# The first chunk of the attention stage: its stream rows in a buffer of their own, its result rows with one load per tile, its statistics tile by tile

## What is computed

```
x = x + 0.5 * ffn(layernorm(x))      # first expert stage
x = x + attn(layernorm(x))           # attention stage
x = x + 0.5 * ffn(layernorm(x))      # second expert stage

def ffn(x):                          # 8 experts, the 2 best of each row
    scores = x @ gate_w.T + gate_b + bias
    top, idx = top_k(scores, 2); gates = softmax(top)
    y_e = silu(x @ w1[e].T + b1[e]) @ w2[e].T + b2[e]
    return sum of gates * y_idx over the two
def attn(x):                         # 6 heads of 128, rows in order of time
    q, k, v = conv4(x @ Wq), conv4(x @ Wk), conv4(x @ Wv)
    alpha, beta = sigmoid(x @ Wa), sigmoid(x @ Wb)
    state = alpha * rotate(state, dq) + beta * rotate(v, k)     # a scan over the rows
    out = rotate(state, -q)
    return (out * rsqrt(mean(out**2)) * rms_w * silu(x @ Wg)) @ Wo
```

## Time and profile before

| | |
|---|---|
| median of 3 runs | 895.51 us (894.84 to 895.96) |
| the profiled execution | 895.87 us |
| its span in the trace | 894.1 us |
| TensorE's mean granted clock | 0.922 of full |
| PE, DVE, ACT, POOL busy | 83%, 70%, 39%, 26% |
| first expert stage ends (last matmul) | 267.5 us from the span's start |
| first matmul of the attention stage | 290.8 us |

### The profile page before, as it was taken

One profiled execution on the slowest core, in us unless ns is written; L12 is line 12 of the kernel. 1 busy time (PEld: TensorE's weight loads), 2 busy tenths in 40 slices (PEclk: granted clock), 3 DMA queues, 4 the chain that ended last, 5 costly groups with the idle time before them and its releaser, 6 DMA issues.

```text
span 894.1 us, 13749 instructions
## 1 busy us (share of the span) xinstructions
PE 737.8 (83%) x4128; PEld 406.8 (45%) x4129; DVE 622.1 (70%) x1009; ACT 348.1 (39%) x600; POOL 236.3 (26%) x222
## 2 busy tenths in 40 slices
PE   8527699999990898997999999999529999999910
PEld 5215455555550444443444444444316565656600
DVE  6886755566654269999989998995775555555545
ACT  5714333434320546445644654532703323333300
POOL 3115644444520101101211011021113434444300
PEclk9859999999995899899999999999859999999965
DMA  9936568865425430610441201363836733333269
GB/s 321 385 111 207 186 223 317 322 243 176 143 83 199 99 89 21 121 49 0 88 78 24 60 12 25 120 166 128 311 112 223 255 107 117 117 106 117 84 223 374
DMA packets 45305, 137.25 MB, mean 153 GB/s; under 512 B 5840, under 2 KB 5840, under 8 KB 41936
## 3 DMA queue, kind: packets, MB, share of 16 engines
q1 hardware_dynamic: 27888, 86.38, 26.8%
q0 software_dynamic: 17376, 50.34, 20.5%
HBM read 85.32 MB, written 51.38 MB: 153 GB/s over the span
## 4 chain that ended last, share of the span: by engine, by line
PE 70%; DVE 15%; DMA 5%; issue 4%; ACT 3%; SPq 1%; POOL 0%; DVEq 0%; POOLq 0%; ACTq 0%
PE bank L615 59%; PE bank L609 4%; PE bank L687 3%; DMA space<-y_rows 2%; PE bank L804 2%; DVE space L1469 1%; DVE space L1466 1%; DVE space L1259 1%; DVE bst L1250 1%; SPq L477 1%; DMA y_rows<-space,slot_dst 1%; DVE space L1316 1%; DMA space<-x_in 1%; DMA space<-xn_rows,slot_src 1%; PE bank L738 1%
## 5 line engine op out<-in xcount | busy, mean ns | idle before, releaser
L615 PE MATMUL bank<-space 128*128 (+3 forms) x2958 | 581.0, 349 | 44.5 <-DVE space L1320 25.6
L615 PEld LDWEIGHTS bank<-space 128*128 128x128 f16 (+1 forms) x2958 | 274.3, 99 | 296.2 <-issue 37.7
L541 POOL DMA_INDIRECT y_rows<-space,slot_dst x78 | 99.7, 1278 | 158.2 <-DVE space L1380 158.2
L1361 DVE TENSOR_TENSOR space<-bank,space 128x512 f16<-128x512 f32 x78 | 54.0, 692 | 84.8 <-issue 43.2
L537 POOL DMA_INDIRECT space<-xn_rows,slot_src x78 | 76.3, 978 | 130.4 <-PE bank L609 70.0
L977 ACT ACTIVATE space<-space 128x352 f32<-128x352 f32 x78 | 38.7, 496 | 177.3 <-DVE space L1367 174.8
L1367 DVE SCALAR_TENSOR_TENSOR space<-bank,space 128x352 f32<-128x352 f32 x78 | 40.9, 524 | 64.0 <-PE bank L615 49.1
L609 PE MATMUL bank<-ident,space 128*128 128x128 f32 x440 | 67.6, 284 | 12.4 <-DMA space<-xn_rows,slot_src 10.5
L982 ACT ACTIVATE space<-bank 128x384 f16<-128x384 f32 x78 | 38.3, 491 | 77.9 <-PE bank L687 76.7
L1380 DVE TENSOR_SCALAR space<-bank,slot_gate 128x512 f32<-128x512 f32 x78 | 58.5, 750 | 12.9 <-PE bank L615 10.3
L1466 DVE SCALAR_TENSOR_TENSOR space<-space,cang 128x512 f32<-128x512 f32 x84 | 63.0, 750 | 5.5 <-ACT space L1051 3.3
(11 more groups left out here) (172 smaller groups left out, 697.4 us busy)
## 6 DMA issues: line engine op xcount, KB each, us to landing
space<-ffn_w SPq DMA_DIRECT2D x8, 1472.0 KB, 10.0
w_saved<-space SPq DMA_DIRECT2D x8, 1472.0 KB
space<-w_saved SPq DMA_DIRECT2D x8, 1472.0 KB, 9.5
space<-y_rows SPq DMA_DIRECT2D x40, 256.0 KB, 6.0
xn_rows<-space SPq DMA_DIRECT2D x8, 1024.0 KB, 6.1
space<-x_in SPq DMA_DIRECT2D x7, 1024.0 KB, 5.3
space<-att_w SPq DMA_DIRECT2D x12, 518.0 KB
space<-y_rows POOLq DMA_DIRECT2D x6, 1024.0 KB, 9.3
```

What stands on the lines that cost most here:

```text
L541: gp.indirect_dma_start(y_rows, bass.IndirectOffsetOnAxis(ap=slot_dst[:, t:t + 1], axis=0), yo[:, t % 2], None).then_inc(y_st[t % 2], 16)
L615: last = pe.matmul(dst, a, b, start=(n == 0), stop=(n == len(terms) - 1))
L1361: v.tensor_tensor(xl[:, par], bank[par][:, :], xh[:, par], ALU.subtract).then_inc(m_xl, 1)
```

## The change

1. Chunk 0's stream rows get a range of their own, `group_rows[0]`, which begins where the second `oh` buffer (odd chunks) begins. The other chunks keep `xgrp`. SP no longer waits for `m_yo` before `group_in(0)`.
2. `y_first` of a tile comes with one load of both result rows (128 x 2 x 512) and not with two.
3. SP issues chunk 1's `group_in` right behind these loads and ahead of `group_out(0)`, without a wait, since `xgrp` isn't used by chunk 0.
4. DVE takes each tile's statistics (`bn_stats`) right behind its two additions.
5. ACT waits for chunk 0's store (`x1_st`) before it first writes the second `oh` buffer, at u = 3.

```diff
+        first_at = lay.at
         oh.append(lay([2 * PAIRS, CH], F16))
         ol.append(lay([2 * PAIRS, CH], F16))
         ...
+        group_rows = [Layout(first_at)([TPC, D])] + [xgrp] * (NCH - 1)
...
             slot_weights()
-            sp.wait_ge(m_yo, SLOT_TILES + 2)
             def group_in(c):
-                sp.dma_start(xgrp, rows4(x_in, c)).then_inc(cg_in, 16)
+                sp.dma_start(group_rows[c], rows4(x_in, c)).then_inc(cg_in, 16)
...
             def next_group_in(c):
-                sp.wait_ge(x1_st, 16 * c)
-                sp.wait_ge(c_xn, TPC * c)
+                if c > 1:
+                    sp.wait_ge(x1_st, 16 * c)
+                    sp.wait_ge(c_xn, TPC * c)
                 group_in(c)
...
             for i in range(TPC):
-                for k in (0, 1):
-                    sp.dma_start(y_first[:, k, i], y_rows[bass.ds(k * T + i * P, P), :]).then_inc(yf_in[i], 16)
+                sp.dma_start(y_first[:, :, i], y_rows[0:2 * T, :].rearrange("(k n p) d -> n p k d", k=2, p=P)[i]).then_inc(yf_in[i], 16)
+            next_group_in(1)
             group_out(0)
-            next_group_in(1)
...
             def gate_high(u):
                 ...
+                if u == PAIRS:
+                    act.wait_ge(x1_st, 16)
...
             def first_rows():
                 v.wait_ge(cg_in, 16)
                 for i in range(TPC):
-                    v.wait_ge(yf_in[i], 32)
-                    seq(v.tensor_tensor(xgrp[:, i], xgrp[:, i], y_first[:, 0, i], ALU.add))
-                    v.tensor_tensor(xgrp[:, i], xgrp[:, i], y_first[:, 1, i], ALU.add).then_inc(c_sum, 1)
+                    v.wait_ge(yf_in[i], 16)
+                    seq(v.tensor_tensor(group_rows[0][:, i], group_rows[0][:, i], y_first[:, 0, i], ALU.add))
+                    v.tensor_tensor(group_rows[0][:, i], group_rows[0][:, i], y_first[:, 1, i], ALU.add).then_inc(c_sum, 1)
                     v.wait_ge(c_sum, i + 1)
+                    ch(v.bn_stats(bst[:, i], group_rows[0][:, i]))
+                ch.wait()
...
             def attention():
                 first_rows()
-                variance(xgrp)
+                moments()
```

More of the change, by code:

```diff
@@ L413, in group_out @@
                     sp.wait_ge(cy_in[1], 16 * c)
-                sp.dma_start(rows4(x_rows, c), xgrp).then_inc(x1_st, 16)
+                sp.dma_start(rows4(x_rows, c), group_rows[c]).then_inc(x1_st, 16)
             def next_group_in(c):
-                sp.wait_ge(x1_st, 16 * c)
-                sp.wait_ge(c_xn, TPC * c)
+                if c > 1:
+                    sp.wait_ge(x1_st, 16 * c)
+                    sp.wait_ge(c_xn, TPC * c)
                 group_in(c)
@@ L1019, in normalise @@
                     act.wait_ge(c_xt, TPC * c + i - 1)
-                act.activation(xnt[:, i % 2], xgrp[:, i], ACT.Identity, scale=rstd[:, 0, 0, i:i + 1],
+                act.activation(xnt[:, i % 2], group_rows[c][:, i], ACT.Identity, scale=rstd[:, 0, 0, i:i + 1],
                                bias=rstd[:, 0, 1, i:i + 1]).then_inc(c_xn, 1)
```

## The result

| | before | after |
|---|---|---|
| median | 895.65 us (894.84 to 896.36, 5 runs) | 891.86 us (891.17 to 892.38, 5 runs) |
| profiled execution | 895.87 us | 891.86 us |
| its span | 894.1 us | 890.1 us |
| TensorE's mean granted clock | 0.922 | 0.919 |

The ratio is 0.9959, with a 95% interval of 0.9947 to 0.9971: the change makes the kernel 3.8 us faster (2.6 to 4.7). I had forecast 891.3 us within 889.2 to 894.0.

A forecast was written before the change was run, and what follows sets the result against it. PE sets the pace, but idles from 267.5 to 290.8 us behind the last scatter and statistics. Gains of 3.54 + 0.7 = 4.24 us take 895.87 to 891.6, forecast as 891.3 against the median, range 889.2 to 894.0.

The forecast's parts named there:

- The last scatter, 3.54 us: First expert stage's end: without chunk 0's load ahead of it, the last `y_rows` scatter takes 3.54 us less, bounds 0 and 3.54.
- The twin: Same last scatter ending the second expert stage, with no load beside it: 2.73 us, used to price the first at 6.27.
- The load's new place, 0: Chunk 0's load behind the last attention weights, about 229.5: PE should not notice, cost 0, at most 1.2 us.
- One load per tile, 0 (0.46 either way): Result rows after the scatter: first tile's data arrives 0.46 us earlier to 0.46 later, taken as 0.
- Statistics tile by tile, 0.7: DVE, first addition to fourth statistics: 8.6 us instead of 9.33, including 0.2 wait; gain 0.7, bounds 0.3 and 1.1.
- The sum: From the experts to the attention: 3.54 + 0.7 = 4.24 us off the path, so the attention starts that much sooner.
- PE, ACT and POOL work behind it only follows: Work after the shortened link: no gain or loss of its own, the attention just starts 4.24 us sooner.
- 2.05 us either way: Rival, PE's clock at the restart after idling: granted earlier (889.3, chance 0.08) or later (893.3, chance 0.09).
- a half-clock stretch more than before: Sign in the changed kernel's profile that would show the prediction wrong: one additional stretch with PE at half clock.
- The scatter's own slowness: Rival: load and scatter share the engines, the scatter is slow for other reasons; gain 1.3 us, 894.2, chance 0.08.
- The stalled experts: Rival: the moved load delays the gather issued at 230.12 and next scatter, costing 7.08 us; 898.3, chance 0.04.

The follow-up runs named there:

- e4: Changed kernel, but SP again waits for the experts' last result before loading chunk 0's stream rows into their own buffer: 893.66 us, ratio 0.9996 to the kernel before.
- e5: Changed kernel with half of chunk 0's stream rows (512 KB) loaded early, the other half behind the experts' last result: 893.52 us, ratio 0.9980 to the kernel before.
- e2: Kernel before with only one load of both result rows per tile: 893.68 us, ratio 0.9995 to the kernel before.
- e7: Changed kernel with 32 added matmuls, results unused, on PE ahead of the attention's first transpose: 889.84 us, ratio 0.9935 to the kernel before.
- e8: Changed kernel with chunk 1's load behind chunk 0's store in SP's queue instead of ahead: 890.27 us, ratio 0.9947 to the kernel before.
- e9: Changed kernel with chunk 0's normalisation factors taken in two halves, tiles 0 and 1, then 2 and 3: 889.25 us, ratio 0.9944 to the kernel before.
- e11: As e9, plus added unused matmuls on PE, 16 ahead of the first transposes and 13 among them: 884.91 us, ratio 0.9897 to the kernel before.
- e12: The changed kernel timed again, unaltered, on another occasion: 889.43 us beside 893.39, ratio 0.9947 to the kernel before.
- e1: Kernel before with only chunk 0's stream rows in their own buffer, loaded early behind the last attention weights: 892.03 us, ratio 0.9972 to the kernel before.
- e3: Kernel before with only the statistics taken tile by tile, two loads per tile kept: 893.35 us, ratio 0.9993 to the kernel before.
- e10: Changed kernel with two loads of result rows per tile again instead of one: 890.99 us, ratio 0.9967 to the kernel before.

## Why the prediction was right, step by step

**The last scatter, 3.54 us.** Right: 6.27 - 2.71 = 3.56. e4 brings the time back with nothing but the load's place, and e5 halves the hold with the load. The twin at the end of the second expert stage was a good price.

**The load's new place, 0.** Right for PE, though the gather's packets were held until 234.5: its margin took that up, and PE was busy for 6.98 of 7.00 us while the engines moved 320 and 377 GB/s.

**One load per tile, 0 (0.46 either way).** In the pair of traces 0.08 later, but over the traces it does cost: with one load the first tile came 3.50 to 4.02 us behind the scatter (after, e2, e4, e5, e7, e8, e9, e11, e12), with two 3.42 to 3.57 (before, e1, e3, e10). The means are 3.84 and 3.50, so the cost is inside the bounds.

**Statistics tile by tile, 0.7.** It was 1.05: the 0.2 us of wait that I had put in for tile 1 did not come, and a tile took 2.05 us, less than the 2.07 to 2.14 of the sum. With two loads the wait is there (0.43 us in e10); what I had not seen is that the one load takes it away, and that the one load alone, without the statistics, would have removed all of the 1.08 (e2). So the two edits of this part overlap, and their gains don't add.

**The sum.** 4.24 forecast; 4.52 from the scatter's issue to the first transposes, 4.40 with the experts' end 0.12 later. The measured gain is 3.79 in the medians and 4.0 in the two profiled executions. The times alone can't tell 4.24 from 3.79 (the interval is 2.6 to 4.7, and e12 has 4.7); the marks in the traces can. The term that they show to be off is the one that I left at nothing: "PE, ACT and POOL work behind it only follows". They follow at the clock that PE is granted. Link and projections took 0.75 + 0.28 us more than before, 1.03 together, since the half-clock stretch now lay over the transposes and the projections' first 3.9 us. It stood among the rivals with 2.05 us either way; it came with half of that. The sign that I had named for it, a half-clock stretch more than before, did not come: between 290 and 308 there is one fewer (before had a second, from 297.8 to 301.2), but the one that is left covers more of PE's work. From 3.38 at chunk 1's statistics the lead went to 4.0 at the end, where the kernels are the same. That the total came within 0.45 us of the forecast is in part luck: 1.03 us was lost to the clock, 0.3 more than forecast was won on the link, and the rest came back where nothing was changed.

**The rivals.** The scatter's own slowness: refuted by e4 and e5, by the amounts, and by the order of the packets. The stalled experts: refuted in the trace of after. The Trainium skill (DMA: Bandwidth & Descriptors, Queues, rings and completion order) has an engine take turns between its queues packet by packet, with typically 9 to 17 descriptors and at most 64 in a packet. The prediction read this as sharing in equal bytes, which I estimate at a hold of 0.64 us that doesn't grow with the load, and the runs show 1.66 and 3.3 to 3.6. With larger turns the rule need not contradict them: the 1 MB load is 512 pieces of 2 KB, an estimate of 32 for each of the 16 engines, and if a piece is a descriptor, all of these could be one turn. No run here shows how many descriptors a turn had. The section's other sentence, that a completion count lands only after every earlier write of the engine, fits the times but isn't needed for them, since the scatter's packets themselves moved late.

**What stays open.** The timed effects of e2 and e3 against the kernel before, and of e9 against e12, are within their intervals. What the matmuls of e7 bring without e9's edit is between 0.4 and 2.1 us by what they are compared with. Why tile 1 came 3.25 us behind tile 0 in e1 has no explanation here. Whether the clock's share in the changed kernel is 1.0 us in the mean, or only in this pair of profiled executions, is not settled: e12, the same code, had its transposes and projections in 7.65 + 32.01 us where the first profile had 7.87 + 33.91, 2.1 us apart.

## What to carry to other kernels

A load that is issued just ahead of a store on which the next stage waits can cost the store the load's whole moving time and more, even from another queue (here 3.56 us for 1 MB that moves in 2.6). Look for its bytes in the stretch between the store's issue and its landing, and put it beside compute, where the DMA engines have room and what stands behind the load in the queues has a margin. When a stage restarts PE after an idle gap, follow the lead from mark to mark: an earlier start at half the clock gives part of it back, there and at later restarts, and the shortened link may show in the time only once matmuls fill the gap (e9 0.2 us, e11 4.5).

## What the runs showed of the hardware

- The hold of a 256 KB indirect scatter by a load that SP had issued 0.20 to 0.25 us earlier went with the load's size: 3.3 and 3.56 us for 1 MB (e4, before), 1.66 us for 512 KB (e5). None of the scatter's 80 packets moved before 273 us, when 442 of the load's had.
- The same 146 matmuls of the projections took 32.01 us at full clock in seven traces (e1, e2, e5, e7, e8, e11, e12) and 33.11 to 34.62 in the others, and the link from the first transposes to them, without the halves, 6.26 to 7.87 us. Identical code (after and e12) fell on both sides. With the correlation of -0.82 between time and clock this speaks for the place of PE's half-clock stretches as a good part of the kernel's noise; no run tests it alone.
- A load of both result rows in one transfer of 512 KB brought the first tile 0.34 us later in the mean than two of 256 KB. The second was there within 1.45 us of the first in e2, where it came 2.49 us behind before; counted from the scatter's landing that is 5.41 us or less, and 5.91.
- Single executions of the kernel before spread over 6 us (890.98 to 897.13 in 35 runs beside e1 to e4, 893.52 to 899.22 in 21 beside e5 to e8), where the 5 runs shown at first stayed within 1.5: five runs say little of the spread.
